# Ternary weight steps laid by an estimate of VectorE's room, instead of evenly, in the scan stage of a two-layer kernel

## The reference, cut to what matters

```
def step(H, inp):
    k_t, v_t, q_t, a_t = inp
    pred = jnp.einsum('bk,bkv->bv', q_t, H)
    err = jnp.sum((v_t - pred) ** 2, axis=-1, keepdims=True)
    surprise = jax.nn.sigmoid(err / (SURPRISE_TEMP + 1e-06))
    kH = jnp.einsum('bk,bkv->bv', k_t, H)
    delta = k_t[:, :, None] * (v_t - kH)[:, None, :]
    H = a * H + (1.0 - a) * (surprise[:, :, None] * delta)
```

```
scale = jnp.clip(jnp.mean(jnp.abs(w_g), axis=-1, keepdims=True), 1e-08, None)
q = jnp.clip(jnp.round(w_g / scale), -1, 1)
w_hat = (q * scale).reshape(w.shape)
return w + jax.lax.stop_gradient(w_hat - w)
```

## Time and profile before

| | |
|---|---|
| median of 3 runs | 1212.82 us (1211.11 to 1213.15) |
| the profiled execution: its own time, its span | 1210.19 us, 1208.1 us |
| busy share of the span: PE, DVE, ACT, POOL | 90%, 72%, 44%, 14% |
| half slots -18 to -1 on VectorE | 28.5 to 73.66 us |
| half slots 0 to 39 on VectorE | 73.66 to 209.75 us |
| granted TensorE clock over the span | 0.93 of full speed |

### The profile page before, as it was taken

The page is one execution under the profiler, slowest core; times in us unless marked ns, Lnnn a source line. Parts: engine busy times, 40 slices in busy tenths (PEclk is TensorE's granted clock), DMA queues, the critical chain, the costliest instruction groups (busy, mean ns, idle before and its releaser), DMA issues. The chain is left out here.

```text
span 1208.1 us, 13011 instructions
## 1 busy us (share of the span) xinstructions
PE 1083.9 (90%) x4345; PEld 525.2 (43%) x4392; DVE 872.7 (72%) x1606; ACT 526.0 (44%) x1100; POOL 169.3 (14%) x143
## 2 busy tenths in 40 slices
PE   6788877689997989898889899999998999999997
PEld 3446633444443444344344354444444444444443
DVE  4887765556665778987779799488897587785654
ACT  4656644235443455435255354154435163531421
POOL 3101000011111322122122122122202000100100
PEclk9857867579999999999999999999999999999999
DMA  8411111413220133323220002013020011020000
GB/s 268 175 53 53 36 36 18 174 41 100 88 87 1 48 126 102 89 64 117 66 84 27 27 27 96 2 44 101 27 69 9 1 53 36 18 70 1 1 35 35
DMA packets 47523, 75.55 MB, mean 63 GB/s; under 512 B 8320, under 2 KB 16000, under 8 KB 47328
## 3 DMA queue, kind: packets, MB, share of 16 engines
q1 hardware_dynamic: 47168, 74.62, 19.6%
q0 software_dynamic: 288, 0.09, 0.2%
HBM read 66.16 MB, written 8.54 MB: 62 GB/s over the span
## 5 line engine op out<-in xcount | busy, mean ns | idle before, releaser
L1491 PE MATMUL g_g<-h,wt 128*128 128x512 f16 x1728 | 402.9, 382 | 5.9 <-DVE hid L1793 2.4
L1491 PEld LDWEIGHTS g_g<-h,wt 128*128 128x128 bf16 (+1 forms) x1728 | 168.5, 99 | 224.6 <-issue 37.1
L1505 PE MATMUL g_d<-wt,parts 128*128 128x512 bf16 (+1 forms) x831 | 200.1, 381 | 7.6 <-DVE tmp L1624 2.7
L2113 ACT ACTIVATE parts<-hid 128x512 f16<-128x512 f32 x108 | 68.2, 631 | 306.9 <-DVE hid L1793 306.9
L1414 PE MATMUL g_o<-shared 128*128 128x512 f32 x384 | 178.5, 608 | 13.6 <-DVE tmp L1585 5.6
L1786 DVE SCALAR_TENSOR_TENSOR hid<-th,g_g 128x512 f32<-128x512 f32 x108 | 73.6, 681 | 125.7 <-ACT th L2106 125.5
L1505 PEld LDWEIGHTS g_d<-wt,parts 128*128 128x128 f16 x864 | 83.8, 99 | 113.5 <-issue 15.7
L2223 POOL TENSOR_TENSOR acc<-acc,sqh 128x512 f32<-128x512 f32 x52 | 76.7, 1475 | 312.9 <-ACT sqh L2119 312.9
L1414 PEld LDWEIGHTS g_o<-shared 128*128 128x128 f32 x384 | 73.2, 194 | 95.1 <-issue 70.1
L1798 DVE TENSOR_TENSOR parts<-hid,parts 128x512 f16<-128x512 f32 x108 | 89.8, 832 | 26.8 <-ACT parts L2113 26.6
L2206 POOL TENSOR_TENSOR g_rstd<-g_var,g_power 128x4 f32<-128x4 f32 x20 | 24.2, 1212 | 328.9 <-DVE g_var L1531 328.9
(11 more groups left out here) (319 smaller groups left out, 1527.7 us busy)
## 6 DMA issues: line engine op xcount, KB each, us to landing
shared<-in_w SPq DMA_DIRECT2D x48, 256.0 KB, 2.7
x<-in_codes SPq DMA_DIRECT2D x32, 264.0 KB, 3.1
w_raw<-in_wt SPq DMA_DIRECT2D x16, 512.0 KB, 3.7
x<-in_wmod SPq DMA_DIRECT2D x7, 1024.0 KB, 5.2
wmod<-in_wmod SPq DMA_DIRECT2D x5, 1024.0 KB, 10.2
codes_f<-x SPq DMA_DIRECT2D x32, 132.0 KB, 1.7
gates<-in_x SPq DMA_DIRECT2D x4, 1024.0 KB, 8.0
x<-in_x SPq DMA_DIRECT2D x4, 1024.0 KB, 6.2
```

The source lines that it names most:

```text
L1491: mm = nc.tensor.matmul(pg[i][:], wide[:, k, o:o + P], h16[f % 2][:, s, k], start=(s == 0 and k == 0), stop=(s == 1 and k == KD - 1))
L1505: mm = nc.tensor.matmul(pd[j][:], parts16[:, t % 3, s, j * P:(j + 1) * P], wd[:, m, :], start=(m == 0 and s == 0), stop=(done and s == 1))
L2113: nc.scalar.activation(parts16[:, t % 3, 0], hid[:, t % 2], ACT.Copy).then_inc(hi_ready, 1)
```

## The change

`room` is, for each half slot from -18 on, a level (1.3 ahead of the scan, 1.9 in it) less `load(h)`, a table entry for each input stage that falls in the slot plus 0.4 for the scan. `share` then gives each half slot steps in proportion to its room. The number of steps stays 112, their order and their instructions stay as they are; the casts and the means move with them, because they use the same function.

```diff
+    LOAD = {0: 0.5, 1: 0.5, 2: 0.5, 3: 0.5, 4: 0.6, 6: 0.5, 7: 0.5, 8: 0.5, 9: 0.5, 18: 0.8, 19: 0.8, 20: 0.5, 21: 0.8, 22: 0.8,
+            23: 0.5, 24: 0.5, 25: 0.5, 26: 0.4, 28: 0.4, 30: 0.4, 32: 0.4}
+    EARLY_LEVEL, LEVEL = 1.3, 1.9
 
     def stages(h):
 
         return [(u, h - BEGIN[u] + 10) for u in range(NG)]
 
+    def load(h):
+
+        n = 0.4 if h >= 0 else 0.0
+        for u, i in stages(h):
+            if u or i >= 10:
+                n += LOAD.get(i, 0.0)
+        return n
+
+    room = {h: max(0.0, (LEVEL if h >= 0 else EARLY_LEVEL) - load(h)) for h in range(TERNARY_FROM, HALVES)}
+
     def share(h, ops):
 
-        h, n = h - TERNARY_FROM, HALVES - TERNARY_FROM
-        return range(max(0, ops * h // n), max(0, min(ops, ops * (h + 1) // n)))
+        whole = sum(room.values())
+        before = sum(n for g, n in room.items() if g < h)
+        return range(round(ops * before / whole), round(ops * (before + room.get(h, 0.0)) / whole))
```

## The result

The change makes the kernel slower: 1226.24 us median of 4 runs (1223.33 to 1227.79) against 1212.99 us of the kernel before on the same chip, a ratio of 1.0096 with its 95% interval [1.0076, 1.0115]; the two medians themselves are 13.3 us, 1.1%, apart. Measured once more later, it was 1225.29 against 1216.26, 1.0061 [1.0037, 1.0086]. The forecast, 1218.6 with a range to 1223.0, had the sign right and less than half of the distance between the first two medians; the time lies outside its range.

A forecast was written before the change was run, and what follows sets the result against it. The prediction saw no single bound: VectorE nearly full in some stretches, a TensorE-VectorE chain in others. Its terms -1.8, +0.15 and +7.5 gave +5.85 us, 1216.0 profiled, 1218.6 on the median, range 1210.5 to 1223 (own range 1215.5 to 1221).

The forecast's parts named there:

- Half slots -18 to 2: Ahead of and at the scan's start: fewer steps and a later cast bring slot 2 earlier, -1.8 us.
- Rival B: Faster: TensorE's clock holds 2.4 GHz in the early part, about -10 ahead of slot 7, total 1210.3 us; chance 0.11.
- Slots 3 to 31: Steps added and removed in these slots nearly cancel: +0.15 us, between -2 and +2.
- slot 24's missing step: Slot 24 loses one step, counted as a gain within the -0.4 us for slots 21 to 29 together.
- slot 21's step: The step added in slot 21 is covered; part of the -0.4 us for slots 21 to 29 together.
- Slots 32 to 39: End of the scan, 25 steps instead of 16, with means and casts: +7.5 us, between 5.3 and 9.7.
- the price of a step: Each VectorE ternary step costs 0.67 us; 687 ns is listed.
- the rule of the even and odd slot: Stages 25 to 32: an even slot's step costs in full, an odd one's is covered while VectorE waits for the product.
- the entry for slot 33: One more step in slot 33; mean (14, 0) in slot 34 waits for it, the product behind: +1.45 us.
- a sign against itself: The forecast is wrong if the means of slots 32 and 34 do not wait.
- rival C: Slower still: slot 35's row and later products run at the low clock, plus casts' upper bound: +9.7, 1222.5 us; chance 0.13.
- The casts' upper bound: Slots 31 to 34: three places each cost the cast put ahead of the gate, 3.1 us instead of 0.9.

The follow-up runs named there:

- e1: The changed kernel with ScalarE's casts two half slots later from slot 26 on, none in 24 and 25: 1.0059 against the kernel before.
- f1: The changed kernel with TensorE's means behind the inputs of their half slot from slot 32 on: 1.0029 against the kernel before.
- e12: The kernel before with the change's 25 steps in slots 32 to 39, nine fewer in slots 10 and 20 to 31, no cast waiting: 1.0069.
- f3: The kernel before with section finish first, 34 early steps, scan steps laid in VectorE's holes, means behind inputs from slot 32: 1202.98 us, 0.9893.
- f2: The kernel before with VectorE's finish of a late section ahead of the odd slot's inputs and steps, second measurement: 0.9971.
- e5: The changed kernel unchanged, measured and profiled a second time: 1225.29 us, 1.0061 against the kernel before.

## Why the prediction was right in sign and short in size

**Half slots -18 to 2, -1.8: right, a little small.** `masked` of slot 2 came at 78.38 us instead of 79.87, the first residual at 71.17 where 70.9 was forecast, slot 2 2.7 earlier by the mean of two. The transfer stayed hidden. What is late next is ScalarE behind VectorE's values, as the step says. But the product that the text had at 50.2 comes at 51.75, no earlier than before, behind a wait of 2.91 us; it gains by taking 0.91 instead of 1.65 us, since the clock falls later. Two errors cancel here. Rival B fell as its "against" said: the clock of 60 to 71.17 us is 0.50 as before, and only 46 to 60 us has 0.75 instead of 0.65. The section of the Trainium skill named there ("TensorE: Matmul & The Clock Gate", "HAM oscillation — how this bites in real kernels") has such a wait bring back the low clock, and the trace agrees: behind the 2.91 us wait the low level begins at 53.1 us.

**Slots 3 to 31, +0.15: the largest miss, 2.6 measured.** That is above the term's own upper bound of +2. Up to slot 12 the terms hold (+1.0 measured by the mean of two, +0.9 forecast). Behind it +1.6 came instead of -0.75. In slots 24 to 31 (+0.5) the step failed that counted slot 24's missing step as a gain: slot 24 is 0.97 us shorter and slot 26 0.9 longer by the mean of two, because the copy for its product stays behind a cast. e1 takes the casts of slots 24 and 25 away, and slot 26 is 1.2 us shorter. The step looked for casts that wait, not for casts in front of something. In slots 12 to 23 (+1.1) the cause stays open: the two profiles of each kernel differ there by 1.1 and 1.4 us. What the rows do show is that slot 21's step was not covered, as the text had it: slot 21 takes 4.71 us in the first profile and 6.23 in the second, 4.38 in both of the kernel before.

**Slots 32 to 39, +7.5: too small, 9.15.** By slots, in the first profiles (8.88 in all), measured against forecast: 32 +0.93 (+0.95), 33 +1.06 (+1.45), 34 +2.23 (+0.65), 35 +2.35 (+1.35), 37 with 38 +0.86 (+0.85), 39 +1.45 (+1.35), and in the casts 0.4 (+0.9) that lies within them. So the price of a step and the rule of the even and odd slot held to some tenths, and the miss is in 34 and 35, 2.6 us. The step that failed is the entry for slot 33: "Mean (14, 0) in slot 34 must wait for it, with the product behind the mean." Those of slots 32 and 34 do not wait at all, which the text had named as a sign against itself. The one that waits is (13, 1) in slot 33, for the step of slot 32, and then (14, 1) in slot 35; behind each stand the transposes. I had looked for the new means of the table, in slots 32, 34 and 38, and not asked of each mean that was already near there whether its step had come closer. f1 shows the price: 2.6 us. One reading of the rows was off as well, without effect on the sum: slot 35's idle time of 5.94 us is not the largest of its chunk, slot 31's is, with 6.22.

**The clock.** The forecast kept TensorE's durations of before in the tail and left its fall to rival C. C was right that the clock costs in the tail and near in size (9.0 us by the mean of two at the end of the scan, 9.7 in C), but the size is in part luck: its 9.7 holds 11.35 for the tail, where 9.15 came. It was wrong on the place: not the wait ahead of the row, which is 1.36 us and not above 3, but that of the mean, two slots earlier. In the change the two waits of slot 35 together, 1.75 and 1.36, are the 3 us that were forecast as one. The casts' upper bound, C's other half, did not come: 0.4 by e12, 0.3 by e1.

**From the sum to the time.** 13.1 us lie between the first profiled executions (1223.33 and 1210.19). 11.2 of these are ahead of the scan's end: the 5.85, the 3.2 us by which the terms were short by the mean of two, and 2.2 that are the luck of these profiles, chiefly the early end of the first of before. 1.9 lie behind, where the instructions are the same. I took one profile's stall pattern for the kernel's, and my own range of 1215.5 to 1221 had no room for it. Of the text's own marks, slot 32's L921 came at 186.40 us (182.4 forecast) and the scan's end at 220.97 (215.6).

## What to carry to other kernels

Idle time of an engine is room for more work only if the work can start inside it: here the holes of 6 us stayed whole, because the steps stood ahead of what TensorE waited for; ask for each hole what would be released later, and move the releaser first (0.3 to 0.8% alone), then the work. Here that gave no more time by itself (0.3 and 0.5%), and 1.1% only once the means, too, stood behind TensorE's other work. When a schedule moves, list every wait whose two ends came closer, on every engine that shares the function, also those of instructions that did not move themselves, and name what stands behind each in its queue. Where the clock can fall, price the new wait with the work behind it at the low level in the forecast itself, and read two profiles of the kernel before ahead of a difference of a few us.

## What was not expected of the hardware

The same eight matmuls of a row took 3.59 us in f3, 4.19 in f2, 5.56 in before and 6.37 in the change, by the granted clock; a pair for the product 0.91, 1.37 and 1.65. In the change 17.1 us at the 1.2 GHz level follow a wait of TensorE of 1.49 us, and TensorE was busy for 13.98 us of them, 82%; e5, e1 and e12, whose mean in slot 33 waits 1.48 or 1.49 us, show the same 17 us. And the same instructions at the same place can keep or lose the clock: slot 27 took 6.28 and 7.50 us in two profiles of the same kernel, and the untouched rest of the program 994.9 to 1003.6 us over all the profiles. That spread goes with the clock: in the two profiles with 994.9 us some 62 us of the rest were granted the low level, in e1 and e5, with 1003.4 and 1003.6, some 81 us.
